# The layers' order of work on TensorE and VectorE: a pair's second weighted values directly behind the first scores, the attention transposes and the variance behind them

## The reference

```
x = x + layernorm(MQA(layernorm(x)))        # one multi-query attention, 16 heads, causal
x = x + layernorm(L(layernorm(x)))          # L: six layers, this is most of the time
for i in range(6):
    s = shift_tokens(x)                      # half of the features come from the token before
    q, k, v = split(s @ Wqkv[i])             # 16 heads of 64, 3 x 1024 columns
    q, k = l2norm(q) * q_scale, l2norm(k) * k_scale, then rotary with xpos scale
    attention in windows of 32 queries on the 64 keys of this window and the one before
    x = out @ Wo[i] + x
    s = shift_tokens(x)
    mu, var over the features; xn = (s - mu) / sqrt(var + 1e-5) * g + b
    a, gate = split(xn @ W1[i] + b1)         # 341 + 341 columns
    x = (a * gelu(gate)) @ W2[i] + b2 + x
```

## Time and profile before

| | us |
|---|---|
| median of 3 runs | 3750.49 |
| lowest, highest | 3749.16, 3756.89 |
| profiled execution, span from its first to its last instruction | 3742.5 |
| PE busy in the profiled execution | 3489.5 (93%) |
| DVE busy | 3020.8 (81%) |
| ACT busy | 2705.2 (72%) |
| POOL busy | 2398.5 (64%) |

### The profile page before, as it was taken

The page is one execution under the profiler, slowest core; times in us unless marked ns, Lnnn a source line. Parts: engine busy times, 40 slices in busy tenths (PEclk is TensorE's granted clock), DMA queues, the critical chain, the costliest instruction groups (busy, mean ns, idle before and its releaser), DMA issues. The chain is left out here.

```text
span 3742.5 us, 161624 instructions
## 1 busy us (share of the span) xinstructions
PE 3489.5 (93%) x67234; PEld 2872.1 (77%) x67234; DVE 3020.8 (81%) x4301; ACT 2705.2 (72%) x4147; POOL 2398.5 (64%) x2884
## 2 busy tenths in 40 slices
PE   6999996699999999999999999999999999999995
PEld 3656554588888888888888888888888888888884
DVE  4556554688889888898888888888888889888884
ACT  2444443478887888878888888888788887878873
POOL 1011011677777777777777777777777777777773
PEclk9999998899999999999999999999999999999997
DMA  1000000132222322222322223222232222222222
GB/s 55 4 3 6 3 3 12 48 90 69 70 70 66 90 69 70 70 61 72 92 71 69 67 69 90 70 69 71 66 90 71 69 70 60 72 66 71 69 65 65
DMA packets 161717, 227.93 MB, mean 61 GB/s; under 512 B 42258, under 2 KB 60632, under 8 KB 161496
## 3 DMA queue, kind: packets, MB, share of 16 engines
q1 hardware_dynamic: 161624, 226.85, 24.2%
HBM read 21.00 MB, written 4.19 MB: 7 GB/s over the span
## 5 line engine op out<-in xcount | busy, mean ns | idle before, releaser
L1184 POOL TENSOR_TENSOR by_cos<-by_cos,by_sin 128x1024 f32<-128x1024 f32 x384 | 910.7, 2382 | 13.6 <-DVE by_sin L1538 13.6
L1190 POOL TENSOR_TENSOR by_cos<-by_cos,norms 128x1024 f32<-128x1024 f32 x384 | 733.5, 1910 | 13.0
L1536 DVE TENSOR_TENSOR by_cos<-proj,turns 128x1024 f32<-128x1024 f32 x384 | 470.2, 1225 | 181.7 <-ACT squares L1426 163.0
L1270 PE MATMUL proj<-qkv_hi,xs_hib 128*128 128x512 f32 x1152 | 512.4, 445 | 49.2 <-DVE by_sin L1538 40.2
L1538 DVE TENSOR_TENSOR by_sin<-proj,turns 128x1024 f32<-128x1024 f32 x384 | 466.3, 1214 | 1.4 <-issue 1.4
L1542 DVE TENSOR_REDUCE sumsb<-squares 128x16 f32<-128x1024 f32 x384 | 464.5, 1210 | 1.5 <-DVE w_lo L1605 1.5
L1272 PE MATMUL proj<-qkv_hi,xs_lob 128*128 128x512 f32 x1152 | 458.3, 398 | 0.0
L1271 PE MATMUL proj<-qkv_lo,xs_hib 128*128 128x512 f32 x1152 | 458.2, 398 | 0.0
L1426 ACT ACTIVATE squares<-proj 128x1024 f32<-128x1024 f32 x384 | 392.7, 1023 | 85.1 <-PE proj L1272 84.7
L1279 PE MATMUL ring<-ident,by_cos 128*128 128x128 f32 x3072 | 385.3, 273 | 8.4 <-DVE xT L1639 5.5
L1406 ACT ACTIVATE vb<-proj 128x1024 f32<-128x1024 f32 x192 | 195.5, 1018 | 255.6 <-DMA v_win<-vb 237.7
(11 more groups left out here) (175 smaller groups left out, 8182.1 us busy)
## 6 DMA issues: line engine op xcount, KB each, us to landing
v_win<-vb SPq DMA_DIRECT2D x1152, 128.0 KB, 2.4
v_win<-vb SPq DMA_DIRECT2D x768, 64.0 KB, 2.0
in_qkv<-L_ffn_Wqkv SPq DMA_DIRECT2D x12, 768.0 KB
wo<-L_ffn_Wo SPq DMA_DIRECT2D x6, 512.0 KB, 4.0
x_tok<-L_attn_x SPq DMA_DIRECT2D x8, 256.0 KB, 4.6
residual<-x_tok SPq DMA_DIRECT2D x8, 256.0 KB, 2.0
o_x<-residual SPq DMA_DIRECT2D x1, 2048.0 KB, 7.7
out<-o_x SPq DMA_DIRECT2D x8, 256.0 KB, 2.3
```

The source lines that it names most:

```text
L1184: nc.gpsimd.tensor_tensor(both, both, by_sin[:, j, :], ALU.add).then_inc(e[f"{w_}_added"].sem, 1)
L1190: nc.gpsimd.tensor_tensor(heads, heads, inverse, ALU.mult).then_inc(e[f"{w_}_ready"].sem, 1)
L1270: nc.tensor.matmul(out, xs_hi[:, tile], qkv_hi[:, cols], start=True, stop=False)
L1536: nc.vector.tensor_tensor(of_heads(by_cos[:, t % 2, j, :]), heads, table(0), ALU.mult)
```

## The change

Two of the five strings change. On PE `V:-1` goes ahead of `O:-2`, directly behind `S:0`; `var` goes behind `Pv:2` and `spread` behind `O:-1`; `Pq:3` goes ahead of `Tq:1`. On DVE `R:-1` goes ahead of `FV`, and `XM` behind `Rk:2`. The strings of ACT, POOL and SP are the same. By the rule of the ring `V:-1` and `O:-2` exchange their buffers: `V:-1` now follows `X:-1`, `O:-2` follows `mean`, `var` follows `V:-1` (so it waits for `R:-1`) and `O:-1` follows `O:-2` (so it waits for `EO:-2`).

```diff
@@ -836,11 +836,11 @@
 CYCLE = {
-    "PE": "V:-2 Pq:2 Tq:0 Tk:0 X:-1 mean Pk:2 S:0 O:-2 V:-1 var Pv:2 spread O:-1 Tq:1 Pq:3 W:-1 Tk:1 Pk:3 GG "
+    "PE": "V:-2 Pq:2 Tq:0 Tk:0 X:-1 mean Pk:2 S:0 V:-1 O:-2 Pv:2 var O:-1 spread Pq:3 Tq:1 W:-1 Tk:1 Pk:3 GG "
     "S:1 AA X:0 Pv:3 F4",
...
-    "DVE": "R:-2 Cq:2 Rq:2 XC RS:-1 Ck:2 FV R:-1 XM Rk:2 MX:0 SB:0 Cq:3 WX:-1 Rq:3 RS:0 Ck:3 AM MX:1 SB:1 Rk:3 "
+    "DVE": "R:-2 Cq:2 Rq:2 XC RS:-1 Ck:2 R:-1 FV Rk:2 XM MX:0 SB:0 Cq:3 WX:-1 Rq:3 RS:0 Ck:3 AM MX:1 SB:1 Rk:3 "
     "XN",
```

## The result

| | before | after |
|---|---|---|
| median of 4 runs, us | 3753.69 | 3853.31 |
| lowest, highest | 3749.16, 3762.15 | 3848.28, 3858.65 |
| span of the profiled execution | 3742.5 | 3847.4 |
| an ordinary cycle of the layers (median of 74) | 30.68 | 31.63 |

The kernel before ran once more beside the changed one, so its median is of 4 runs here. The ratio is 1.0268, with a 95% interval of 1.0248 to 1.0288. The forecast was 3827, its range ended at 3852; the direction and the mechanism were right, the size was 27% too small on the span (77 forecast, 104.9 measured), and the median lies 1.3 above the range.

What follows compares the result with a forecast made beforehand. PE's string, busy 93% of the span, was taken to set the cycle. 95 cycles at 0.82 gave 78, borders -4 and +3, so +77 on 3742.5; with 8.0 to the median, 3827 us, range 3790 to 3852.

Steps and rivals of the forecast that it cites:

- PE's string is the cycle: PE has no gaps but block changes, so reordering only cheapens seams or opens waits; nothing gives the 0.82 back.
- The seams: On PE, S ahead of V costs 1.35 (1.28 to 1.42); without waits a cycle would be 0.23 shorter.
- `Pv:2`, `var`: Pv:2 waits 0.12 for DVE's Ck:2 and starts at 5.33; var, waiting for R:-1, at 6.87, counted from Pk:2.
- `spread`: On PE, waits 0.28 for POOL by a 1.61 chain from var; starts at 8.48, Pq:3 0.13 later at 8.61.
- ACT's order decides: Qq:3 queues behind EQ:1 on ACT; PE waits 0.60 and Pk:3 starts at 15.81 against 14.99.
- the sum: 95 cycles give 78, borders -4 and +3: together +77 on the span of 3742.5, so 3819.5.
- The term of 0.82 a cycle: Pk:3 starts 0.82 us later in each of 95 cycles, making 78.
- The borders: At five layer borders, w_lo's DVE work hides ACT's wait (-4); Pv:2's wait for DVE loses the earlier gain (+3).
- The median: The median of the runs stays 8.0 above the profiled span, so 3827.5.
- A: S:0 to Pq:3: the seam wins and the waits don't come, -0.23 a cycle, 3729; chance 0.04.
- B: Next cycle's waits, X:-1 on EQ:0 and Pk:2 on Cq:2, take up half: +0.41 a cycle, 3789; chance 0.06.
- C: POOL late too: Mk:1 ends behind 15.0 and Tk:1 becomes the bound, about 1.2 a cycle, 3864; chance 0.06.

Runs made afterwards that it cites:

- 4: Changed kernel with the waits of V:-1, and PE's semaphore increment, made ahead of S:0: ratio 1.0221 to the kernel before, cycle 31.51 us.
- 8: Changed kernel with Qq:3 ahead of EQ:1 and IG:2 on ACT, V:-1's waits ahead of S:0, POOL's power replaced by a constant: ratio 0.9993, cycle 30.58.
- 1: Kernel before with one edit, Pq:3 ahead of Tq:1 on PE: ratio 1.0257, cycle 31.73 us.
- 2: Changed kernel with Qq:3 moved ahead of EQ:1 and IG:2 on ACT: ratio 1.0120 to the kernel before, cycle 31.01 us.
- 5: Changed kernel with Qq:3 ahead of EQ:1 and IG:2 on ACT and V:-1's waits made ahead of S:0: ratio 1.0111, cycle 30.90 us.
- 9: Changed kernel, Qq:3 ahead of EQ:1, V:-1's waits ahead of S:0, Pq:3 cut in two around spread: ratio 1.0067, cycle 30.79 us.
- 6: Kernel before with only the waits of O:-2 made ahead of S:0, order untouched: ratio 1.0007, cycle 30.69 us.
- 7: Kernel before with Pq:3 ahead of Tq:1 on PE and Qq:3 ahead of EQ:1 and IG:2 on ACT: ratio 1.0119, cycle 31.12 us.
- 3: Changed kernel with Tq:1 ahead of Pq:3 on PE again: ratio 1.0279 to the kernel before, cycle 31.77 us.

## Why the prediction was right and where it was wrong

**PE's string is the cycle, and a wait opened in it is paid in full.** Right: nothing behind `Pk:3` gave anything back; in the changed kernel `Pk:3` to the next `Pk:2` takes 15.71, before it was 15.69.

**The seams.** I took 1.35 for `S` ahead of `V`, between 1.28 and 1.42; it is 1.41, because of the semaphore instructions (4). At `Pv:2` it cost nothing, since that is held by `Ck:2` at 5.32. But it was not free, as my working had it from there on: 4 shows that `O:-2`, `R:-1` and `var` hang on it as well, and that without it the cycle is 0.12 shorter.

**`Pv:2`, `var`.** Right to 0.01: 5.32 and 6.87.

**`spread`.** The chain from `var` is 1.65, I had 1.61 from the earlier trace rows; the seam to `Pq:3` is 0.20, I had 0.13. The 0.13 holds where `spread` does not wait (8: 0.14), so here the block behind one that waited starts 0.06 later. I had added such a tail to none of the waits. Together these make `Pq:3` 0.11 late, and with it `Pk:3`.

**ACT's order decides.** Right, with its size: 7.20 from `Pq:3` to `Pk:3` in 1 and in the changed kernel, forecast 7.20, and 0.62 gained back by the one edit in 2.

**The step that failed is the sum.** The mechanism held, its terms were too small. The term of 0.82 a cycle measured 0.95 (`Pk:3` 0.12 later, and the block behind it another 0.01): over 75 ordinary cycles 9.5 us. The borders were mis-sized: I gave their 15 cycles 15 x 0.82 - 1 = 11.3, they took 17.9. The ends were not worked out at all, which put them at the term of an ordinary cycle without a reason: 7.2 instead of 2.5 for the first five cycles (of which three had the term), 7.0 instead of 0.8 for the last four. With the odd cycle (0.6 less than its term) and the 1.6 ahead of the layers, these parts make up the 28 us that were missing on the span.

Of the ends the runs show where they come from in part. The last four cycles take 7 us more in the changed kernel, 5 to 6 more in 2 to 5 and 9, 1.5 more in 8 and nothing more in 1, 6 and 7. So this cost came with the moves of `V:-1`, `O:-2` and `var` and the wait for POOL, not with the swap. In the first five cycles the kernels differ without such a pattern (7.2 in the changed kernel, 5.6 in 1, 1.8 in 3, 0.9 in 8). TensorE's granted clock was lower at both ends of the changed kernel: 0.80 against 0.88 before from 650 to 780 us, and 0.81 against 0.84 from the last four cycles to the end of the program. How much of the ends is due to the clock is open.

At the borders two things went wrong. I had let the 0.8 disappear in the cycle with `w_lo`; it got 0.49 longer. ACT's wait did disappear there, but DVE itself was late: `w_lo` stands behind `XM`, which the new order puts behind `FV` and `Rk:2`, and `FV` waits for `var`. `w_lo` itself took 2.27 instead of 1.90. From there to `Cq:3`, the last row, DVE has no wait for another engine, and it starts 14.87 behind `Pk:2`, before 14.38:

```profile
1282.32 0.16 DVE L1621 TENSOR_SCALAR f_varb<-ring 128x2 f32<-128x2 f32 x1 [0.97 <-PE ring L1349]
...
1284.19 2.27 DVE L1605 TENSOR_TENSOR w_lo<-in_w,w_hi 128x768 fp32r<-128x768 f32 x1
...
1289.11 1.22 DVE L1536 TENSOR_TENSOR by_cos<-proj,turns 128x1024 f32<-128x1024 f32 x1
```

The other is the cycle in which `Pv:2` waits for `lo_v1` on VectorE. I had it at 0.82 + 0.6 = 1.42. It got 1.4 longer at two borders, as forecast, and 2.6 at the other three. The difference between these two is in the granted clock. The first stretch is such a cycle from the start of `Pv:2`, the second one of the shorter kind:

```profile
1698.00:1701.50 3.50, 3.30 (x11) 2.78 (x12) 1.28 (x3) 0.59 (x1) 0.00 (x0) 0.59 0.70 166
1186.00:1189.00 3.00, 2.89 (x21) 2.43 (x20) 2.01 (x5) 2.18 (x3) 1.88 (x2) 1.00 0.66 161
```

The figure behind the five engines is PEclk: 0.59, a mix of the two levels, against 1.00. Ahead of it PE had stood still behind `O:-2`:

```profile
1698.20 0.50 PE L1270 MATMUL proj<-qkv_hi,xs_hib 128*128 128x512 f32 x1 [2.01 <-DVE by_sin L1538]
...
1699.33 0.63 PE L1270 MATMUL proj<-qkv_hi,xs_hib 128*128 128x512 f32 x1
...
1700.61 0.85 PE L1349 MATMUL ring<-mean_of,fsqb 128*128 128x1 f32 x4
```

By bringing `V:-1` and `O:-2` forward, the change turned a wait of about 1.6 in this place into one of 2.2 in one piece, and at three of five borders the granted clock fell to 0.5, its lower level, for 3.4 us. The longer wait alone does not explain this. In 3 the same wait of 2.2 stands at all five borders and the clock stays full; in 4 it falls at one of five. In 1, whose order in the cycle is that of the kernel before up to this place, the wait is 1.6 as there, and yet the clock falls at three of five borders, 1.3 to 1.5 us behind the start of `Pv:2`; in the kernel before and in 6 it falls at none. The first row is from 1, the second from 3:

```profile
1179.00:1183.00 4.00, 4.00 (x17) 3.47 (x17) 2.69 (x5) 1.72 (x2) 2.94 (x3) 0.57 0.73 172
1699.00:1703.00 4.00, 2.86 (x18) 2.43 (x18) 3.04 (x4) 1.24 (x2) 0.58 (x1) 1.00 0.62 154
```

So what decides is open; each kernel was profiled in one execution only. TensorE: Matmul & The Clock Gate in the Trainium skill, section HAM oscillation — how this bites in real kernels, describes waits for data between bursts of matmuls that put TensorE back to its lower clock. The trace agrees at three of the five borders of the changed kernel, where a wait of 2.2 came before the fall; the five such waits in 3 had no fall behind them.

**The median.** I put the runs 8.0 above the span. The profiled execution of the changed kernel was timed at 3849.16, 1.8 above its span of 3847.4; the rest of such a distance is the spread between runs. Here the median came out 5.9 above.

**The rivals.** A (the seam wins) is out: with the waits at `var`, `spread` and `Pk:3` taken away and the seam at its best, 8 is 0.10 a cycle ahead of the kernel before, not 0.23; `Pv:2` still waits at 5.32. B is out, nothing was given back. C is out for an ordinary cycle: `Tk:1` has no wait in the changed kernel. It has one, 0.57 by the profile's bracket, in the cycle with `w_lo`, where POOL waits for that, but there `Pk:3` is held by DVE for longer. The rule that ACT can't overtake is borne out by 2.

## What to carry to other kernels

When each engine runs its own fixed string, a swap of two steps on one engine has to be followed on every engine that reads their results: ask for each consumer which of the two inputs it now waits for first, and what stands behind that wait. A seam is worth moving blocks for only if it was measured for the very pair of blocks; here the new order was worth 0.1 us a cycle once all its waits were gone (8), and the waits that it brought cost ten times that. In a forecast, the ends and borders of a pipeline have to be worked out by themselves: here they took 32 us, where under 15 were forecast.

## What the runs showed of the hardware

- Two blocks of 64*32 matmuls run into each other (1.19 us from start to start instead of 1.41, matmuls of both in between each other) if no semaphore instruction stands between them (4); with the waits and the increment between them the seam is 1.41, as long as that to the whole array. Which of the instructions does it was not separated.
- The seam from 64*32 pieces to the whole array stayed at 1.41 when the waits between the two were taken away (6).
- The block behind `spread` started 0.20 behind it where `spread` had waited (the changed kernel), 0.14 where it had not (8).
- In the midst of a stage that otherwise ran at full clock, the granted clock fell to 0.5 for 3.4 us behind some waits of PE and not behind others of the same length and in the same place: a wait of 2.2 us was followed by it in three of five cases in the changed kernel, in one of five in 4 and in none in 3, a wait of 1.6 us in three of five in 1 and in none in the kernel before. The length of the wait alone does not decide it.
